# Loading and casting the first pair of attention weights through four staging buffers, behind the first block of x

## The reference

```python
def elu_feature_map(x): return jax.nn.elu(x) + 1.0
# attention
q = elu_feature_map((x @ Wq.T).reshape(B, S, H, hd))
k = elu_feature_map((x @ Wk.T).reshape(B, S, H, hd))
v = (x @ Wv.T).reshape(B, S, H, hd)
KV = jnp.einsum('bshd,bshe->bhde', k, v)
out = jnp.einsum('bshd,bhde->bshe', q, KV)
z = jnp.einsum('bshd,bhd->bsh', q, k.sum(axis=1))[..., None]
attn = (out / (z + EPS)).reshape(B, S, D) @ Wo.T
x = _layernorm(x + attn)
# feed-forward, integer weights times 1/127
h = jax.nn.silu(x @ wg.T) * (x @ wu.T)
x = _layernorm(x + h @ wd.T)
```

## Time and profile before

| | us |
|---|---|
| median of the two timed runs | 1932.76 |
| the two timed runs | 1906.74 and 1958.78 |
| the profiled execution, its own time | 1893.74 |
| its span on the slowest core (core 6) | 1892.2 |
| spans of the eight cores | 1877.7 to 1892.2 |

### The profile page before, as it was taken

One profiled execution on the slowest core, in us unless ns is written; L12 is line 12 of the kernel. 1 busy time (PEld: TensorE's weight loads), 2 busy tenths in 40 slices (PEclk: granted clock), 3 DMA queues, 4 the chain that ended last, 5 costly groups with the idle time before them and its releaser, 6 DMA issues.

```text
span 1892.2 us, 22903 instructions; the slowest of 8 cores (1877.7 to 1892.2 us)
## 1 busy us (share of the span) xinstructions
PE 1549.3 (82%) x7277; PEld 685.0 (36%) x7424; DVE 514.2 (27%) x971; ACT 554.8 (29%) x809; POOL 42.4 (2%) x44
## 2 busy tenths in 40 slices
PE   0368654767899899989897887899899989989998
PEld 0123321322344344434343333344344444434443
DVE  0024242112421332133112334311432232233111
ACT  2343212211252234214222331432252234114213
POOL 0002001111000000000000000000000000000000
PEclk9989887899999999989998999899999999989999
DMA  4799527787255334512654442445145435522431
GB/s 142 199 279 319 128 95 211 206 255 257 75 126 155 90 103 138 152 38 73 206 153 104 85 88 89 123 129 151 55 112 163 116 84 131 153 62 63 138 107 45
DMA packets 213236, 255.28 MB, mean 135 GB/s; under 512 B 136320, under 2 KB 136320, under 8 KB 212096
## 3 DMA queue, kind: packets, MB, share of 16 engines
q1 hardware_dynamic: 213120, 253.81, 47.7%
HBM read 184.55 MB, written 37.75 MB: 117 GB/s over the span
## 4 chain that ended last, share of the span: by engine, by line
PE 65%; DMA 15%; DVE 7%; ACT 6%; issue 4%; SPq 1%; POOL 1%; DVEq 0%; another core or an unknown queue 0%; ACTq 0%; POOLq 0%
PE ps_c L712 18%; PE ps_a L1104 15%; PE ps_b L1117 15%; PE ps_b L917 5%; PE ps_a L544 2%; PE ps_b L530 2%; DVE t L805 2%; PE ps_a L530 2%; DMA outb<-wui 2%; PE ps_b L544 2%; ACT texp L812 2%; DMA scr_wu<-wgu 2%; PE ps_a L793 2%; DVE q_fm L819 2%; DMA outb<-wgi 2%
## 5 line engine op out<-in xcount | busy, mean ns | idle before, releaser
L1117 PE MATMUL ps_b<-ln1T,wgu 128*128 128x512 bf16 x1507 | 367.9, 385 | 37.7 <-DVE h_fm L1144 36.2
L1104 PE MATMUL ps_a<-ln1T,wgu 128*128 128x512 bf16 x1505 | 364.5, 382 | 28.0 <-ACT silu_b L1136 9.5
L712 PE MATMUL ps_c<-wd_buf,h_fm 128*128 128x512 bf16 x1503 | 351.3, 390 | 2.1 <-issue 0.4
L1136 ACT ACTIVATE silu_b<-ps_a,consts 128x512 bf16<-128x512 f32 x192 | 131.2, 687 | 538.5 <-PE ps_a L1104 442.2
L1144 DVE SCALAR_TENSOR_TENSOR h_fm<-ps_b,silu_b 128x512 bf16<-128x512 f32 x192 | 131.9, 691 | 485.3 <-PE ps_b L1117 452.4
L1117 PEld LDWEIGHTS ps_b<-ln1T,wgu 128*128 128x128 bf16 x1536 | 150.6, 99 | 226.2 <-issue 52.9
L1104 PEld LDWEIGHTS ps_a<-ln1T,wgu 128*128 128x128 bf16 x1536 | 150.8, 99 | 214.2 <-issue 38.6
L712 PEld LDWEIGHTS ps_c<-wd_buf,h_fm 128*128 128x128 bf16 x1536 | 153.0, 100 | 185.7 <-issue 19.4
L917 PE MATMUL ps_b<-wpair,attnT 128*128 128x512 bf16 x499 | 131.9, 421 | 32.0 <-DVE res L940 14.2
L616 ACT ACTIVATE texp<-res 128x1024 bf16<-128x1024 f32 x64 | 67.3, 1052 | 298.4 <-DVE res L735 237.5
L793 PE MATMUL ps_a<-xT,wpair 128*128 128x512 bf16 x500 | 126.5, 399 | 32.0 <-DVE q_fm L819 26.0
(11 more groups left out here) (56 smaller groups left out, 803.2 us busy)
## 6 DMA issues: line engine op xcount, KB each, us to landing
wgu<-scr_wg SPq DMA_DIRECT2D x168, 256.0 KB, 2.7
wgu<-scr_wu SPq DMA_DIRECT2D x168, 256.0 KB, 2.7
x_f<-x SPq DMA_DIRECT2D x56, 512.0 KB, 4.5
out<-outb SPq DMA_DIRECT2D x32, 512.0 KB, 2.8
outb<-wgi SPq DMA_DIRECT2D x24, 512.0 KB, 5.1
outb<-wui SPq DMA_DIRECT2D x24, 512.0 KB, 5.2
outb<-wdi SPq DMA_DIRECT2D x12, 512.0 KB, 7.8
wgu<-wdi SPq DMA_DIRECT2D x12, 512.0 KB, 8.4
```

The lines of the kernel that those rows point to most:

```text
L712: t.matmul(d_view[:, pr, hl * 512:(hl + 1) * 512], h_fm[:, hm, sc * 128:(sc + 1) * 128], wd_buf[:, hm, hl * 512:(hl + 1) * 512], start=(hm ...
L1104: t.matmul(ps_a[:, (m % 2) * 512:(m % 2 + 1) * 512], wgu[:, 0, r, j * 128:(j + 1) * 128], ln1T[:, j, :], start=(j == 0), stop=(j == NJ - 1)),
L1117: t.matmul(ps_b[:, (m % 2) * 512:(m % 2 + 1) * 512], wgu[:, 1, r, j * 128:(j + 1) * 128], ln1T[:, j, :], start=(j == 0), stop=(j == NJ - 1)),
L1136: e.activation(silu_b[:, m % 2, :], ps_a[:, (m % 2) * 512:(m % 2 + 1) * 512], AF.Silu, scale=consts[:, 2:3]),
```

## The change

`load_pair_direct` is rewritten and moved. The 16 loads are the same in size and source. They alternate between Wk and Wv, go through four staging buffers (the two of `x_f32` and the two of `outb`) with four slots, and their casts alternate between ScalarE (Wk) and VectorE (Wv). Each slice has its own `Track`, and each of the first block's matmuls waits for its own slice. The call comes after the first block's x load, cast and transpose instead of ahead of them. The other users of `wpair` take the new tracks; in `load_pair`, `pair_st` and the later matmuls every track of a matrix carries the same token.

```diff
-        tr_wpair = [Track() for _ in range(2)]
+        tr_wp = [[Track() for _ in range(NJ)] for _ in range(2)]
...
         def load_pair_direct(m0, m1):
-            for si, mat in enumerate((m0, m1)):
-                fsrc = w_imgs[mat]
-                for j in range(NJ):
-                    r = j % 2
-                    ld = P.dma(f"wp{si}",
+            stg4 = [x_f32[:, 0, :], x_f32[:, 1, :], outb[:, 0, :], outb[:, 1, :]]
+            trs4 = [tr_x[0], tr_x[1], tr_outb[0], tr_outb[1]]
+            for j in range(NJ):
+                for si, mat in enumerate((m0, m1)):
+                    idx = 2 * j + si
+                    r = idx % 4
+                    fsrc = w_imgs[mat]
+                    ld = P.dma(f"wp{r}",
                                lambda s, fsrc=fsrc, j=j, r=r:
-                               s.dma_start(x_f32[:, r, :], fsrc[:, j * D:(j + 1) * D]),
-                               waits=[tr_x[r].begin_write()], eng=BULKQ)
-                    tr_x[r].end_write(ld)
-                    ct = P.op("scalar",
+                               s.dma_start(stg4[r], fsrc[:, j * D:(j + 1) * D]),
+                               waits=[trs4[r].begin_write()], eng=BULKQ)
+                    trs4[r].end_write(ld)
+                    ct = P.op("scalar" if idx % 2 == 0 else "vector",
                               lambda e, si=si, j=j, r=r:
-                              e.activation(wpair[:, si, j, :], x_f32[:, r, :], AF.Copy),
-                              waits=[ld, tr_wpair[si].begin_write() if j == 0 else None])
...
+                              (e.activation(wpair[:, si, j, :], stg4[r], AF.Copy)
+                               if hasattr(e, "activation") else
+                               e.tensor_copy(wpair[:, si, j, :], stg4[r])),
+                              waits=[ld, tr_wp[si][j].begin_write()])
+                    trs4[r].add_reader(ct)
+                    tr_wp[si][j].end_write(ct)
...
         def phase1(s, first):
-            if first:
-                load_pair_direct("wk", "wv")
             NCH = SEQ // 128
...
             load_x_tp(cts.pop(0), order[0] % CPT)
+            if first:
+                load_pair_direct("wk", "wv")
...
-                            waits=[tr_xT[tq].reads(), tr_wpair[0].reads()]
+                            waits=[tr_xT[tq].reads(), tr_wp[0][j].reads()]
...
-                            waits=[tr_xT[tq].reads(), tr_wpair[1].reads()]
+                            waits=[tr_xT[tq].reads(), tr_wp[1][j].reads()]
```

More of the change, by code:

```diff
@@ L330, in drain_w_jobs @@
                                                "p a b -> p (a b)")),
-                               waits=[tr_wpair[si].reads()], eng=BULKQ)
-                    tr_wpair[si].add_reader(st)
+                               waits=[t.reads() for t in tr_wp[si]],
+                               eng=BULKQ)
+                    for t in tr_wp[si]:
+                        t.add_reader(st)
                     for t in tr_scr[mat]:
@@ L421, in load_pair @@
                                        scr_qkvo[mat][:]),
-                           waits=[tr_wpair[si].begin_write()]
+                           waits=[t.begin_write() for t in tr_wp[si]]
                                  + [t.reads() for t in tr_scr[mat]],
                            eng=BULKQ)
-                tr_wpair[si].end_write(ld)
+                for t in tr_wp[si]:
+                    t.end_write(ld)
         xring = [0]
@@ L552, in phase1 @@
                 tr_xT[tq].add_reader(tok)
-                tr_wpair[0].add_reader(tok)
-                tr_wpair[1].add_reader(tok)
+                for j in range(NJ):
+                    tr_wp[0][j].add_reader(tok)
+                    tr_wp[1][j].add_reader(tok)
                 if u > 0:
@@ L795, in phase2 @@
                                  xT[:, j, :], start=(j == 0), stop=(j == NJ - 1)),
-                        waits=[tt.reads() for tt in tr_xT] + [tr_wpair[0].reads()]
+                        waits=[tt.reads() for tt in tr_xT] + [tr_wp[0][j].reads()]
                               + (bw((abk,)) if j == 0 else []),
@@ L920, in emit_c2 @@
                                      start=(e_ == 0), stop=(e_ == NJ - 1)),
-                            waits=[tr_attnT[tc].reads(), tr_wpair[1].reads()]
+                            waits=[tr_attnT[tc].reads(), tr_wp[1][e_].reads()]
                                   + (bw(("b0", "b1")) if (e_ == 0 and hl == 0) else []),
```

## The result

| us | before | after |
|---|---|---|
| median of all timed runs | 1932.76 (10 runs) | 1872.78 (11 runs) |
| lowest | 1895.84 | 1868.89 |
| profiled execution | 1893.74 | 1871.17 |
| its span, mean of the eight cores | 1885.7 | 1863.7 |

The ratio of the undisturbed runs is 0.9851, with an interval of 0.9830 to 0.9872: the changed kernel is faster, by 1.5%, and that is clear of the noise. (In some executions one half of the chip ran at a lower granted clock throughout, as in the 1939 us of the changed kernel, with 0.90 on four cores and 0.94 on the others; the ratio leaves out such long runs, 1958.78 among them, and "undisturbed" means the rest.) The medians are over all runs, so their difference of 60 us is not the gain; the lowest differ by 27. The forecast was 1874 us and a gain of 26 us.

What follows compares the result with a forecast made beforehand. The prediction held that single 512 KB weight transfers, one in flight, bound the first 56.7 us. x first and four in flight gain 26.3 us, other parts zero, giving 1874 us; own range 1860 to 1889, extended to 1850 to 1915.

Steps and rivals of the forecast that it cites:

- What bound the kernel: First 56.74 us: round trip of single 512 KB weight transfers sets the pace, at 139 GB/s and DMA share 0.46.
- The sum: Start of everything from the second x load on: 54.5 - 16 x 1.76 us, 26.3 us earlier; casts, tracks, buffers zero.
- The term s: Time one 512 KB weight transfer occupies full DMA engines: 1.76 us taken, from 298 GB/s; considered values 1.27 to 2.27.
- the starting point: Base time before subtracting the gain: profiled 1893.7 or shorter timed run 1906.7, giving 1867.7 or 1880.4; middle taken, 1874 us.
- x first: First x load at 1.06 us, ahead of the weights: transpose issued at about 7.95, first weight load at 9.4 us.
- Casts and per-slice waits at nothing: Weight stage and block 0: VectorE casts hidden under transfers, per-slice matmul waits shorten nothing on the path; both zero.
- The gain reaches the end: Everything from the second x load on starts 26 us earlier, keeping its length; 1647 us from SP's load of Wq from scratch.
- No change: Rival: weight loads do not overlap, 3.5 us each, gain -1.5 us, about 1900 us; within the 0.08 for under 18 us.
- eaten by the next stage: Rival: weight traffic drags the transpose or x load, Wq loads start late; 18 us gain, 1882; within 0.08 for little gain.
- The clock: Rival: TensorE's ragged early work lowers the clock to 1.2 GHz through blocks 6 to 15, costing 72 us, 1940; chance 0.04.
- The larger gain: Rival: weight stage and first block's matmuls gain more, beyond 2% needing 38 us, about 1851 us; chance of over 34 us 0.08.
- within 2%: Verdict on whole-kernel time: change under 2%, about what measurement cannot tell from none; chance 0.82.

Runs made afterwards that it cites:

- the two controls: Kernel before and changed kernel, both unaltered, profiled again on one chip: SP's load of Wq from scratch at 242.6 and 216.0 us, ratio 0.9851.
- the first two profiles: First profiled executions of the kernel before and the changed kernel: SP's load of Wq from scratch at 242.8 and 219.6 us, mean of eight cores.
- the control: Changed kernel unaltered, profiled again on the chip of the all-ScalarE-casts, whole-matrix-waits and six-buffer runs: SP's load of Wq from scratch at 216.0 us, ratio 0.9851.
- whole waits: Changed kernel with block 0's matmuls waiting for all eight slices of their matrix: SP's load of Wq from scratch at 215.7 us, ratio 0.9856.

## Why the forecast was right in size and wrong in its verdict

*What bound the kernel.* Right. The wait for the slot set the pace, not memory or casts: removing it alone gave 15 us, putting it back took everything. With it gone, the buffers are the next limit: with two of them SP waits for casts and the marker is at 228, with four it is at 216.

*The sum.* The size was right: 26.3 us worked out; measured at the marker 26.6 between the two controls and 23.3 between the first two profiles; 1874 us forecast, 1872.8 measured. The term s can be read by itself, as a sixteenth of the time from the issue of the first weight load to that of x block 1 (mean of the eight cores): 8.74 to 37.52 in the control, 1.80 us a slice, and 8.86 to 39.29 in the first profile, 1.90, against the 1.76 taken. So 16 s came out 0.6 and 2.2 us longer than forecast, inside its bounds of 1.27 and 2.27 and in the first profile near the 1.93 which the rounds of the down weights gave. The full stretches show the same: a share of 0.95 at 283 GB/s in the first profile and 0.96 at 292 in the control, both under the 298 of the row, which lasted 5 us. What neither row could show is the filling: the stretch from 9.09 to 12.90 runs at 149 GB/s, and the first slice lands only at 16.1, so that TensorE starts at 17.45 and not at about 13 as forecast; x block 1 is issued while the last slices are still in flight, so the filling is not added to the stage. That 1874 was hit to 1.2 us is in part luck: two executions of the changed kernel differ by more at the marker, and the starting point was a choice between two values (below).

The Trainium skill, DMA: Bandwidth & Descriptors, section Specifications, puts a core's part of the memory at about 358 GB/s; the estimate from that page was a gain of 31.1 us. With 283 to 294 GB/s in the full stretches of the slowest cores and gains of 23.3 and 26.6 us, the traces of these runs do not agree with it for this stage.

*x first.* The transpose was issued at 7.68 (forecast 7.95), the first weight load at 9.09 (9.4), the second x cast at 43.1 to 44.2 (43.5). The sum moved the chain of x from behind the weights to ahead of them at the same price, so the move itself was worth nothing in it. The runs with x last bear that out within their 3 us.

*Casts and per-slice waits at nothing.* Right, both. VectorE's cast took 0.69 us where the nearest row said 0.70.

*The gain reaches the end.* Right: 1643 us behind the marker against the forecast 1647 (which was core 6's alone), and the next stage kept its length. Cut at the same distance from the markers, the slowest core of each control shows nearly the same rows for the loads of Wq and Wo and for the 184 us behind the pass. The control of the kernel before, and then that of the changed kernel:

```profile
66.00:134.60 68.60, 44.99 (x208) 18.24 (x208) 12.31 (x12) 29.52 (x29) 0.97 (x1) 0.83 0.95 256
...
242.60:426.60 184.00, 114.46 (x476) 45.98 (x474) 50.09 (x96) 36.34 (x55) 21.85 (x21) 0.82 0.69 198
```

```profile
40.00:108.00 68.00, 43.07 (x189) 17.13 (x190) 13.69 (x14) 30.37 (x30) 1.04 (x1) 0.82 0.92 262
...
216.00:400.00 184.00, 114.55 (x471) 46.10 (x470) 51.41 (x96) 36.95 (x56) 21.84 (x21) 0.81 0.68 201
```

*The rivals.* "No change" fell with the two slots. The gain was not eaten by the next stage, as the two pairs of rows show. The clock, which would have made it slower, did not come: 0.82 against 0.83 in the stretch that follows and 0.81 against 0.82 in the 184 us after the pass, and the key groups of 16 matmuls take 3.61 us from 111.83 on, where in the first profile of the kernel before they do from 137.36 on. The larger gain fell with the six buffers: deeper than four gives no more. The granted clock of the kernel before in 40 slices, on which that rival stood; that of the changed kernel is under the result:

```profile
PEclk9989887899999999989998999899999999989999
```

*The step that failed* is the one that turned the sum into a verdict: "A difference under 2% is about what a measurement of this kernel cannot tell from none; the forecast's 1.4% lies inside", and with it 0.82 on "within 2%", which reads as no change. To the letter 1.5% lies within 2%; the reading of it as none is what the runs refute. The undisturbed runs of the changed kernel lie between 1868.9 and 1875.4, 0.35% apart, the five timed ones of the kernel before between 1895.8 and 1906.7, 0.6% apart (in later jobs up to 1.1%), and the interval of the ratio is 0.4% wide; 1.5% stands well clear of one. I had taken the 2.7% between the two runs shown as the spread of a measurement, when the longer of them is one that the ratio leaves out, and had widened the range to 1915 for it. Within the sum lay the better statement: the whole of the forecast's own range, 18 to 34 us, is a gain, and it held 0.80 of the chance, so "faster, by about 1.4%" was what the working said.

The starting point was a guess too, the middle between 1893.7 and 1906.7, which is 1900.2. The undisturbed runs of the kernel before in the same job have a median of 1899.0; in the later jobs it was 1897.1, 1894.6, 1897.2 and 1904.4.

## What to carry to other kernels

When an engine's queue waits for its own transfers, count how many may be in flight by the semaphores, not by the buffers; here two buffers behind one slot name had a depth of one, and a changed name gave 15 us. Take the price of a fuller queue from a stretch of the same trace where the DMA share is already near one, and expect the gain to stop there: depth 1, 2, 4 and 6 put the marker at 243, 228, 216 (220 in another execution) and 215 us. Where a one-time stage lies ahead of a long steady one, read its gain at markers inside the trace, the nearest one above all: at the second x cast 4 us could be told apart over several executions, where the time of the whole kernel could not do it.

## What the runs showed of the hardware

The matmuls that go in pairs between two landings are slow. The group of block 0's key matmuls in the changed kernel, TensorE from 0 to 50 us (count, busy us, mean ns, idle before and releaser), keeps TensorE busy for 8.1 us with 16 matmuls of 609 ns each, two of which overlap in a pair. A group of 16 from 111.83 on is busy for 3.61 us with matmuls of 378 ns, each overlapping the next. The granted clock of both stretches reads 1.00:

```profile
L535 PE MATMUL ps_a<-wpair,xT 128*128 128x512 bf16 x16 | 8.1, 609 | 35.7 <-ACT wpair L413 35.7
```

Some of it can be the end of a pair, which nothing follows. But the value matmuls behind them, 16 in a row, took 5.30 us instead of 3.62 too. Slow groups are not peculiar to pairs: the first group after each long idle stretch took 4.97 to 5.62 us in the kernel before, at 1.00 in the earlier trace rows for the first of them, and the values right behind it 3.62. With whole waits it was the same, 5.49 and then 3.62. So a full group of keys brought the next group to full pace, and eight pairs did not. They cost nothing here, but work that is moved under loads in drops should be priced at up to 2.2 times its duration (8.1 against 3.61), and the row of the granted clock does not show it in this trace.

Also not expected: the fourth load behind a transpose held SP for 2.26 us, and in the kernel with six buffers the fifth and sixth took 1.47 and 0.94; with the three early loads ahead of the transpose, none of the ring's loads took SP over 0.6 us. The ring's later loads in the changed kernel take 0.33 us each to issue.
